# Attention scores as nine bf16 products of exact thirds, stacked on array rows through device memory

## What is computed

```python
q, k, v = jnp.split(ctx @ wi.T + bi, 3, axis=-1)          # 16 heads of 8 features
scores = jnp.einsum('bhqd,bhkd->bhqk', q, k) / sqrt(8)
attn   = softmax(scores, axis=-1)
o      = einsum('bhqk,bhkd->bhqd', attn, v)  ->  @ wo.T + bo
h = ctx + o;  x1 = layernorm(h) * ln1g + ln1b
# route every token to one of 8 experts (two softmaxes, argmax), run its MLP,
out = layernorm(x1 + weight * expert(x1)) * ln2g + ln2b + x
```

## Time and profile before

| | us |
|---|---|
| median of 3 runs | 566.42 |
| profiled execution, its own time | 565.99 |
| its span in the profile | 564.2 |
| of this PE busy | 499.3 (88%) |
| DVE busy | 423.8 (75%) |
| ACT busy | 393.3 (70%) |
| POOL busy | 286.2 (51%) |

### The profile page before, as it was taken

How to read it: one execution, slowest core, us unless ns; L and a number is a source line. 1 busy time by engine, 2 the same in 40 slices (tenths; PEclk the granted TensorE clock), 3 DMA queues, 4 the chain that set the end, 5 groups by cost and what they waited for, 6 DMA issues and landing times. The chain is left out here.

```text
span 564.2 us, 14442 instructions
## 1 busy us (share of the span) xinstructions
PE 499.3 (88%) x4663; PEld 338.0 (60%) x4663; DVE 423.8 (75%) x1192; ACT 393.3 (70%) x1144; POOL 286.2 (51%) x511
## 2 busy tenths in 40 slices
PE   5998899999999999999789999999997867697880
PEld 3765566667767777765345656565564555576760
DVE  3589988888888888987455688787878768765652
ACT  3567688888888887787466778776876537476750
POOL 0587653322222222020345458887887375755673
PEclk9999999999999999999999999999999899978895
DMA  8700999999995000000100000101041043243310
GB/s 350 290 3 1 303 301 297 294 296 288 292 297 145 0 0 0 2 1 1 37 3 2 1 3 21 39 31 39 31 189 39 25 142 102 90 118 103 102 33 5
DMA packets 48535, 60.90 MB, mean 108 GB/s; under 512 B 2488, under 2 KB 45509, under 8 KB 47574
## 3 DMA queue, kind: packets, MB, share of 16 engines
q1 hardware_dynamic: 45686, 53.72, 32.7%
q0 software_dynamic: 2784, 6.37, 3.2%
HBM read 18.43 MB, written 42.10 MB: 107 GB/s over the span
## 5 line engine op out<-in xcount | busy, mean ns | idle before, releaser
L1619 DVE TENSOR_REDUCE nm<-SC 128x8 f32<-128x1024 f32 x64 | 75.4, 1219 | 29.8 <-PE SC L1115 29.4
L2146 ACT ACTIVATE room_p<-ST 128x512 f32<-128x512 f32 (+1 forms) x96 | 64.2, 742 | 23.8 <-PE ST L1133 23.8
L1515 DVE TENSOR_REDUCE room_w<-SC 128x512 f32<-128x2048 f32 x32 | 73.1, 2284 | 1.3 <-PE SC L945 1.3
L613 POOL TENSOR_TENSOR spread<-parts,units 128x48 bf16<-128x48 bf16 x32 | 8.8, 275 | 122.3 <-DVE parts L1490 122.3
L2053 ACT ACTIVATE room_w<-room_w,shift 128x128 f32<-128x128 f32 x128 | 50.0, 393 | 17.8 <-DVE shift L1524 17.8
L812 POOL DMA_INDIRECT out<-room_v,id_r x39 | 39.4, 1009 | 25.0 <-DVE room_v L1967 18.1
L2044 ACT ACTIVATE room_w<-ST,cv 128x128 f32<-128x128 f32 x128 | 36.6, 368 | 18.2 <-PE ST L960 18.1
L960 PEld LDWEIGHTS ST<-room_w 128*128 128x128 f32 x256 | 33.1, 191 | 15.3 <-issue 13.0
L2062 ACT ACTIVATE room_w<-room_w,inv 128x128 f32<-128x128 f32 x128 | 41.2, 410 | 0.0
L715 POOL DMA_INDIRECT sorted_rows<-room_w,slot_i x32 | 33.4, 1042 | 14.0 <-issue 9.7
L913 PE MATMUL ST<-room_w 128*128 128x136 f32 x256 | 40.2, 279 | 0.0
(11 more groups left out here) (307 smaller groups left out, 1367.3 us busy)
## 6 DMA issues: line engine op xcount, KB each, us to landing
sorted_rows<-w SPq DMA_DIRECT2D x8, 4290.0 KB, 38.4
room_v<-sorted_rows SPq DMA_DIRECT2D x39, 130.0 KB
x_t<-xT SPq DMA_DIRECT2D x2, 1024.0 KB, 8.2
ctx_t<-adj SPq DMA_DIRECT2D x1, 2048.0 KB, 16.8
room_w<-x SPq DMA_DIRECT2D x8, 256.0 KB, 3.0
room_w<-mask SPq DMA_DIRECT2D x1, 1536.0 KB
w<-weights SPq DMA_DIRECT2D x1, 1356.0 KB, 8.8
x_t<-w SPq DMA_DIRECT2D x1, 1032.0 KB, 5.0
```

The lines of the kernel that those rows point to most:

```text
L1515: dve.tensor_reduce(logit[:, :, :], SC[:, :, :].rearrange("p b (i m) -> p b m i", i=TYPES), AX_X, ALU.max)\
L1619: dve.tensor_reduce(nm[:, v % 2, 2 * PER_R * pair:2 * PER_R * (pair + 1)], SC[:, 2 * pair:2 * pair + 2, :].rearrange("p r (i n) -> p (r i) ...
L2146: act.activation(ex[:, v % 2, first:last, :], ST[:, first:last, :], ACT.Exp)\
```

## The change

Groups 1 to 7 get new score products; group 0 keeps the masked float32 ones.

1. **Thirds.** A value of q or k is split exactly in three bf16 parts: HIGH (the upper two bytes), MID (the upper bytes of the rest), LOW (what is left). HIGH and MID are copied by ScalarE (`high_part`, `mid_part`), the rest and LOW are two POOL subtractions (`lower_parts`); VectorE does group 1's keys (`first_lower_parts`).
2. **Stacking.** SP writes the parts to device memory, 8 DMAs of 128 KB for a group's queries and 8 for its keys (`stage`), waits for them, and reads them back so that a strip of 32 rows holds four parts of one head (`stack`: 2 DMAs of 512 KB for each operand, and 4 of 32 KB for the keys' lows). The head order changes to 4i + r.
3. **Products.** `scores` and `turned_scores` of a batch are each 3 x 4 x 4 = 48 bf16 matmuls of 32 (or 8) rows by 128 columns, four strips in turn, instead of 4 float32 matmuls of 32 rows by 512.
4. **Removed:** `mask_keys`, both `mask_queries`, `rows_x`.
5. **Rows of x early.** After the rounds SP loads all of x (2 MB) into the room of the mask, POOL adds ln2b (8 instructions), SP writes it to device memory as `biased_rows`; `load_rows` reads from there.
6. **Order.** Queries and keys of group 1 are projected in step -2 and `scores(1)` waits for `key_ready` 2; later `query` at the first, `key` at the third, `value` at the fourth batch of a group. `load_rows(g-2)` stands in SP's queue after the stacking of group g (from g = 4); the experts' weights are loaded after group 2's. Half of the first 13 tile loads may start before the last scores.

```diff
+            def stage(x, g, part):
+                for a, s in PLACES[x, part]:
+                    sp.dma_start(score_parts[g % 2, x, a, :, :, s, :, :].rearrange("i r c n -> (i r) c n"),
+                                 part_s[:, x, part, :]).then_inc(S("staged_k" if x else "staged_q"), 16)
+            def stack(x, g):
+                sp.wait_ge(S("staged_k" if x else "staged_q"), STAGED * g)
+                if g == 1:
+                    sp.wait_ge(v_evac, 2 * STEPS)
+                    sp.wait_ge(plpc_done, STEPS)
+                else:
+                    sp.wait_ge(S("st_mm"), 2 * GB * (g - 1))
+                for a in range(2):
+                    sp.dma_start((k_st if x else q_st)[:, g % 2, a, :, :],
+                                 score_parts[g % 2, x, a].rearrange("i r s c n -> (r s c) i n")).then_inc(S("stacked"), 16)
+                if x == KEY:
+                    for r in range(ROWS_R):
+                        sp.dma_start(low_st[STRIP * r:STRIP * r + HD, g % 2, :, :],
...
+            load_rows(0)
+            load_rows(1)
+            for g in range(1, G):
+                stacked_queries(g)
+                stacked_keys(g)
+                if g == 2:
+                    sp.wait_ge(mu_done, STEPS)
+                    sp.wait_ge(ctx_done, STEPS - G)
+                    sp.dma_start(w1_s, w1).then_inc(S("in_experts"), 16)
+                    sp.dma_start(w2_s, w2).then_inc(S("in_experts"), 16)
+                if g >= 4:
+                    load_rows(g - 2)
             load_rows(6)
...
             def scores(v):
...
+                if g > 0:
+                    if b == 0:
+                        pe.wait_ge(S("stacked"), STACKED * g)
+                    cols = slice(b * N, (b + 1) * N)
+                    for a in (LOWS, 1, 0):
+                        for i in range(PER_R):
+                            last = a == 0 and i == PER_R - 1
+                            for r in range(ROWS_R):
+                                mm = pe.matmul(SC[:, r, i * N:(i + 1) * N], stacked_q(g, a, r, i, cols),
+                                               stacked_k(g, a, r, i, cols), start=(a == LOWS and i == 0), stop=last)
...
             def lower_banks_free(u):
...
+                if u == -1:
+                    pe.wait_ge(S("key_ready"), 2)
...
             def pieces(u):
...
+                if u == -2:
+                    query(1, Y0)
+                    key(1, Y1)
+                if b == 0 and far:
+                    query(later, Y0)
+                if b == 2 and far and u > 0:
+                    key(later, Y0)
+                if b == 3 and more and nxt > 0:
                     value(nxt, Y0)
...
+                if u == -2:
+                    query_out(1, Y0)
+                    key_out(1, Y1)
+                if u == 0:
+                    mid_part(QUERY, 1)
+                    mid_part(KEY, 1)
+                if b == 0 and far:
+                    query_out(later, Y0)
+                    high_part(QUERY, later)
+                if b == 2 and far and u > 0:
+                    key_out(later, Y0)
+                    mid_part(QUERY, later)
+                if b == 3 and far and u > 0:
+                    high_part(KEY, later)
+                    mid_part(KEY, later)
```

More of the change, by code:

```diff
@@ L208, in build @@
         w2_s = Bf(128, EXPERTS * FF)
+        rows = Bf(128, 2, GB, ROW)
         v_a = Bf(128, 2, GB, VROW)
@@ L498, in load_rows @@
                     sp.wait_ge(S(f"scattered{p % 2}"), 16 * GB * (p // 2))
-                sp.dma_start(rows[:, p % 2, :, D:2 * D], x_rows[:, p * GB:(p + 1) * GB, :])\
+                sp.dma_start(rows[:, p % 2, :, D:2 * D], biased_rows[:, p * GB:(p + 1) * GB, :])\
                     .then_inc(S(f"in_rows{p % 2}"), 16)
[L501 to L506, removed]
@@ new lines, in stacked_queries, with stacked_keys @@
+            def stacked_queries(g):
+                if g > 2:
+                    sp.wait_ge(S("stacked"), STACKED * (g - 2))
+                sp.wait_ge(S("parts_high"), act_part(g, "qh"))
+                stage(QUERY, g, HIGH)
+                sp.wait_ge(S("parts_low"), pool_part(g, "ql"))
+                stage(QUERY, g, LOW)
+                sp.wait_ge(S("parts_high"), act_part(g, "qm"))
+                stage(QUERY, g, MID)
+                stack(QUERY, g)
+            def stacked_keys(g):
+                sp.wait_ge(S("parts_high"), act_part(g, "kh"))
+                stage(KEY, g, HIGH)
+                if g == 1:
+                    sp.wait_ge(S("km_ready"), 2 * PER_R + 2)
+                else:
+                    sp.wait_ge(S("parts_low"), pool_part(g, "kl"))
+                stage(KEY, g, LOW)
+                sp.wait_ge(S("parts_high"), act_part(g, "km"))
+                stage(KEY, g, MID)
+                stack(KEY, g)
@@ L752, in _ @@
             for u in FLOW:
-                nxt, b, more = group(u, 1)
+                later, b, far = group(u, 2)
                 norm, _, normed = group(u, -2)
@@ L1254, in pieces @@
                     pe.wait_ge(S("ex_ready"), 3 * u + 1)
-                if b == 0 and more:
-                    query(nxt, Y0)
-                if b == 1 and more:
+                if u == -2:
[5 more added lines that the diff above has]
+                    key(later, Y0)
+                if b == 3 and more and nxt > 0:
                     value(nxt, Y0)
-                if b == 3 and far:
-                    key(later, Y0)
                 if u == -1:
@@ L1879, in _ @@
                         residual_out(u - 4)
-                    if b == 1 and more and nxt > 0:
+                    if b == 3 and more and nxt > 0:
                         value_out(nxt, Y0)
```

219 lines of the change are left out of this document (131 added, 88 removed).

## The result

The changed kernel takes 629.3 us against 567.5 us for the kernel before on the same chip: 1.109 times (95% interval 1.106 to 1.113), 61.8 us slower. The forecast was 585.8 us, with a range up to 598: the sign was right, the size was not. The profiled execution has a span of 627.6 us (564.2 before), so 63.4 us are to be found.

A forecast was written before the change was run, and what follows sets the result against it. Bound: a loop of PE's turned scores, ACT's exponentials, then PE again. Start +3.4, group 1 +7.4, groups 5 to 7 +12.7, clock +2.0, products -5.0, DVE -0.7 give +19.8: 585.8 us, range 561 to 598.

The forecast's parts named there:

- Part 1: Score products of groups 1 to 7: bf16 blocks of 0.72 us against 0.94, steps of 5.52 us, -5.0 us.
- Part 2: Engine work: POOL's changes worth nothing, ACT's extra copies taken at 0, two DVE additions dropped for -0.7 us.
- The -0.7 us behind the heads: Two DVE additions of 0.68 us each go away behind the heads: -0.7 us (0 to -1.4).
- Part 3: Start: projections ahead of scores(1) cost 2.8 us, ACT's extra work in step 0 another 0.6: +3.4 us.
- Part 4: Group 1's round trip: operands land at 296.9 us, so batch 4's scores stall 7.4 us (4.9 to 8.6).
- The longer landing: Waits for stores: a fixed DMA cost of about 2.0 us makes each 0.6 us longer; not used in the sum.
- Part 5: Round trips of later groups: groups 5 to 7 stall 12.7 us (7.0 to 19.9), groups 2 to 4 fit.
- The wait on the scatter: SP's load of rows waits for group g-4's scatters, 3.8 us into the step, with the next group's chain behind it.
- Part 6: PE's clock halves after stalls, four of them: 2.0 us lost, between 0 and 6.4.
- The prediction's own sign: Steps of groups 2 to 4 longer than 5.7 us would prove it wrong, pointing to the array or ACT.

The follow-up runs named there:

- the pair without trips: Changed kernel, rows' load later and ACT's waits moved, without stores or loads of thirds: 1.018; also with POOL's subtractions held until DVE's row tops: 1.005.
- the fillers: Changed kernel with useless float32 matmuls on PE ahead of its waits for stacked operands: 1.094, where the changed kernel had 1.109.
- one trip: Changed kernel storing and loading thirds for group 1 only, later groups reusing its operands: 1.026 with 48 products a block, 1.023 with 12.

## Why the prediction was wrong

- **Part 1, the products: right.** A block takes 0.68 us (0.72 forecast), an undisturbed step 5.34 us, and without trips and without the blocked DVE the heads gain 4.5 us, 0.18 us a step from batch 4 to 28. The rule of the Trainium skill ("TensorE: Matmul & The Clock Gate", Wait — 56ns, not 53.3ns?), no starts closer than 25 ns, would make 1.2 us of them; 48 starts within 0.64 us say that it does not bind strips side by side.
- **Part 2, POOL at nothing: failed, though it cost little here.** It priced POOL's new subtractions by the time that POOL has. What they cost is DVE's time at their new places, 0.7 to 0.9 us each time that they meet. Without trips this happened six times and turned 134.0 into 138.5 us (shown by the pair without trips). In the changed kernel itself only two such instructions are long (0.93 and 1.04 us), for one before, so there it is worth some 1 us.
- **The -0.7 us behind the heads: 0 on the first chip.** On the others the part behind the heads is 91.5 us with the rows early alone, for 93.7.
- **Part 3, the start: +2.8 us forecast up to batch 0, +3.1 measured; +0.6 forecast in step 0, +3.9 measured.** Of the 3.1 us, 0.8 come with the rows' early load (the run with it alone), which the forecast had called free. Step 0 took 9.1 us for 5.2, for `staged_q` ahead of `query_out(2)` was missed.
- **Part 4, group 1: 7.4 us forecast, 6.0 measured, for the wrong reasons.** The operands came 3.9 us later than forecast: the queries' stores had landed 1.9 us late, the keys' 3.1 us, and the keys' loads took 7.0 us for 6.1. A store was issued every 0.65 us for 0.45, and the landings came 2.3 and 2.9 us behind the last issue (283.16 to 285.48, 290.92 to 293.85), where the sum had 1.7 and 1.3. The longer landing that the prediction set beside its row, by the Trainium skill ("DMA: Bandwidth & Descriptors", Anatomy of one DMA), came nearer; the page gives its 2.0 us for transfers that GpSimd issues, and these are SP's. PE came late as well (idle from 294.8, not 289.5). With that delay gone the stall is 10.0 us.
- **Part 5, the step that failed most plainly. Groups 5 to 7: 12.7 us forecast, 18.9 measured, and groups 2 to 4 were ruled out and cost 7.1.** The wait on the scatter was found, and with the load moved (and group 1's stores reordered) the ratio went from 1.109 to 1.056, the largest step of all. Wrong was "a group's loads may start at the turned scores of step 4g-5, and need about 13.5 us where three steps give 17.7". The keys' parts are ready to be stored only 4 us into that step, and from there group 3 took 17 us in the first trace (337.0 to 354.1). And the projection that starts the chain stands behind the stalled scores, so that a stall is handed on.
- **Part 6, the clock: 2.0 us forecast, the worst of the sizes.** It was taken from one stretch of the earlier trace rows with 3.3 us at half clock. The 65 us measured have up to 21 us in them; the fillers gave about 8 back, with overlapping intervals.
- **Not in the sum at all: PE's instruction supply.** Twice the instructions, in half the time each: 11.8 us of issue waits on the first chip for 2.3, and 7.4 on the second. The prediction's own sign, steps of groups 2 to 4 over 5.7 us, did show (5.9 to 6.6 us in most steps without a stall), but it had named the array or ACT for it, and blocks of 0.68 us rule out the array.

So the heads' +60.3 us are 32.0 of stalls, 9.5 of issue waits, up to 21 of half clock, some 3 of ACT's wait in step 0, less 1 to 5 for the products. These overlap and leave a few microseconds either way. Against the forecast's +19.8 that is 12 us more of stalls, up to 19 of clock, 9.5 of issue waits with no term at all, and some 3 in step 0. The forecast's upper bound did not hold since each term had a range of its own, and none for what one stall does to the next or for PE's instructions.

## What to carry to other kernels

A chain of store, wait and load on one queue is priced from the instruction that makes its last input to the landing of its last load, with the issue time of that very access pattern; then look at what stands behind the stalled instruction, for that is often the start of the next chain. Idle time of the matrix engine can be paid twice, once as idle and once as half clock: here 6 us idle, then 4 us of work at 0.50. And an instruction moved to an idle engine still needs a port: look at what its neighbour does in that microsecond, not at the share of busy time.

## What the runs showed of the hardware

- A GpSimd subtraction with SBUF operands holds up a DVE cast or two-input instruction of 8 to 16 elements until it ends: 0.90 to 1.04 us for 0.17 to 0.18. DVE's reduction from PSUM beside it stayed at 2.35 us for the pair.
- PE stands (up to 3.4 us) with nothing to wait for in the profile when blocks of 48 short matmuls and their weight loads run beside heavy DMA traffic: 7.4 us in the heads, but 1.8 us with one trip, and 0.2 us with a quarter of the products. Ten kernels with the trips and 48 products had from 2.5 to 11.8 us. That instructions were missing, and that their loads queue behind the data, is inferred from these and one slow load.
- SP starts a store of 128 KB with a three-dimensional pattern in device memory every 0.65 us, against 0.48 between the two loads L506 and L507 of the earlier trace rows, and so a row of such stores moves about 200 GB/s at most.
- The part behind the heads takes 110.4 us on one chip and 93.7 us on another, for the same kernel before, and the heads 179.7 and 179.3 us.
- Forty-eight bf16 matmuls of 128 columns, on four strips in turn, start within 0.64 us (311.72 to 312.36).
